# Unrolled attention with three slots for q and k, and eight-head layers in three bf16 parts

## The reference

```
attn = softmax(q @ k.T * scale)        # 1024 x 1024, no mask
out  = attn @ v                        # width 16 (8 heads) or 8 (16 heads)
```

## Time and profile before

| | us |
|---|---|
| median of 3 runs | 3769.32 |
| lowest and highest | 3768.4 and 3776.37 |
| profiled execution, own time | 3765.51 |
| its span in the profile | 3763.8 |
| PE busy in the span | 3126.6 (83%) |
| DVE busy | 2793.6 (74%) |
| ACT busy | 1868.8 (50%) |
| POOL busy | 438.7 (12%) |

### The profile page before, as it was taken

The page is one execution under the profiler, slowest core; times in us unless marked ns, Lnnn a source line. Parts: engine busy times, 40 slices in busy tenths (PEclk is TensorE's granted clock), DMA queues, the critical chain, the costliest instruction groups (busy, mean ns, idle before and its releaser), DMA issues. The chain is left out here.

```text
span 3763.8 us, 61047 instructions
## 1 busy us (share of the span) xinstructions
PE 3126.6 (83%) x19914; PEld 1782.2 (47%) x19914; DVE 2793.6 (74%) x4370; ACT 1868.8 (50%) x3233; POOL 438.7 (12%) x495
## 2 busy tenths in 40 slices
PE   6758898848888889847898979958999777759998
PEld 4533333422222223333333457656777544447776
DVE  5658877389888888547777434469999776679998
ACT  2215767517877778614767611214444444424443
POOL 0140000040000000050000001031222000032222
PEclk9857989868999999956989868859999888859999
DMA  0051212030000111041222010011111000011111
GB/s 25 15 123 25 42 29 46 5 95 16 31 30 31 33 32 40 1 95 45 46 47 46 2 24 1 0 46 46 45 45 45 4 1 0 9 52 45 45 45 53
DMA packets 74816, 131.97 MB, mean 35 GB/s; under 512 B 13872, under 2 KB 30288, under 8 KB 74576
## 3 DMA queue, kind: packets, MB, share of 16 engines
q1 hardware_dynamic: 74576, 128.75, 14.1%
HBM read 85.72 MB, written 25.43 MB: 30 GB/s over the span
## 5 line engine op out<-in xcount | busy, mean ns | idle before, releaser
L728 DVE TENSOR_REDUCE nested_a_halves<-banks 128x2 f32<-128x1024 f32 x512 | 615.9, 1222 | 132.7 <-PE banks L834 129.6
L728 DVE TENSOR_REDUCE wide_a_halves<-banks 128x2 f32<-128x1024 f32 x512 | 594.7, 1218 | 80.8 <-PE banks L834 80.5
L784 ACT ACTIVATE nested_a_p<-banks 128x512 f32<-128x512 f32 x1024 | 554.5, 597 | 201.2 <-PE banks L858 184.7
L784 ACT ACTIVATE wide_a_p<-banks 128x512 f32<-128x512 f32 x1024 | 554.1, 598 | 89.0 <-PE banks L858 66.9
L1678 ACT ACTIVATE mix_e_h<-banks,mix_b_folded 128x512 f32<-128x512 f32 x512 | 353.5, 690 | 391.8 <-PE banks L1691 383.7
L1642 DVE TENSOR_TENSOR mix_e_h_low<-mix_e_h,mix_e_h_high 128x512 fp32r<-128x512 f32 x512 | 464.0, 906 | 17.5
L834 PE MATMUL banks<-nested_k_stack,nested_q_stack 48*128 48x512 f32 x1024 | 283.0, 547 | 88.8 <-DMA nested_q_stack<-nested_q_parts 46.5
L872 PE MATMUL banks<-nested_a_p,nested_v 128*32 128x256 f32 x4096 | 345.9, 419 | 0.0
L872 PE MATMUL banks<-wide_a_p,wide_v 128*32 128x256 f32 x4096 | 333.1, 404 | 11.1 <-issue 11.1
L858 PE MATMUL banks<-nested_q_stack,nested_k_stack 50*128 50x512 f32 x1024 | 262.1, 444 | 10.1 <-ACT nested_a_p L784 9.6
L834 PE MATMUL banks<-wide_k_stack,wide_q_stack 48*128 48x512 bf16 x1024 | 211.7, 410 | 59.1 <-issue 18.5
(11 more groups left out here) (367 smaller groups left out, 4575.3 us busy)
## 6 DMA issues: line engine op xcount, KB each, us to landing
mix_e_gate<-mix_gates_t SPq DMA_DIRECT2D x128, 256.0 KB, 3.2
nested_q_stack<-nested_q_parts SPq DMA_DIRECT2D x96, 128.0 KB
nested_q_parts<-nested_p_q_cut SPq DMA_DIRECT2D x16, 512.0 KB
nested_k_parts<-nested_p_k_cut SPq DMA_DIRECT2D x16, 512.0 KB
nested_k_stack<-nested_k_parts SPq DMA_DIRECT2D x32, 256.0 KB
nested_v<-nested_values SPq DMA_DIRECT2D x16, 512.0 KB, 10.1
wide_v<-wide_values SPq DMA_DIRECT2D x16, 512.0 KB, 3.0
wide_q_stack<-wide_q_parts SPq DMA_DIRECT2D x192, 32.0 KB
```

The costliest lines, as they stand in the source:

```text
L728: dve.tensor_reduce(halves[:, half, i, 2 * a:2 * a + 2], bank[:, at:at + 2, :], AX, ALU.max).then_inc(maxed, 1)
L784: act.activation(p[:, kt % 4, j, :], bank[:, ST + n % RING, :], ACT.Exp, scale=scale).then_inc(probs, 1)
```

## The change

The loops of the attention stage become straight code over all units. `q_stack` and `k_stack` get three slots, the tile `v` and its copies go, and PE reads the values from `values`. SP loads group u/2 + 2 at the even unit u once all shifted scores of the units before u are done, and issues `shift_load(u)` behind it. The nested layers use bf16 in three parts: `pairs = [3, 2, 1]` with a width of 16 is 96 rows, 98 with the shift rows, so the span becomes 128, `per_tile` 1 and `slabs` 4. A load is then 3 + 6 = 9 DMAs per group in the nested layers, 18 in the wide one (before: 10 and 18, and one for `v`).

```diff
 class Heads:
     GROUP = 4
+    SLOTS = 3
...
-        self.q_stack = core.sbuf(ctx, "q_stack", [P, 2, self.slabs, T], kind)
-        self.k_stack = core.sbuf(ctx, "k_stack", [P, 2, self.slabs, T], kind)
-        self.v = core.sbuf(ctx, "v", [P, 2, TILES, self.GROUP * 32])
+        self.q_stack = core.sbuf(ctx, "q_stack", [P, self.SLOTS, self.slabs, T], kind)
+        self.k_stack = core.sbuf(ctx, "k_stack", [P, self.SLOTS, self.slabs, T], kind)
...
-                src = self.k_parts[bass.ds(n, 1), :, h, 0:count].rearrange("o s c e t -> (c e) (o s) t")
+                src = self.k_parts[n, :, h, 0:count].rearrange("s c e t -> (c e) s t")
...
-        sp.dma_start(self.v[:, k], self.values[:, bass.ds(n, 1)].rearrange("p o i c -> p (o i) c")).then_inc(
-            self.v_in[k], 16)
...
-                sp.wait_ge(v_copied, 2 * hd.groups)
-                for k in range(2):
-                    hd.load(sp, k, k)
+                for n in range(2):
+                    hd.load(sp, n)
...
-                shift_load(0, 0)
                 sp.wait_ge(hd.parts_out, 32 * hd.parts * B)
-
-                def turn(it, first, last):
-                    for ui in range(4):
-                        u, k = it * 4 + ui, ui // 2
-                        if ui % 2 == 0 and not (first and k == 0) and not (last and k == 1):
-                            sp.wait_ge(mixed, u * TILES)
-                            hd.load(sp, it * 2 + k + 1, (k + 1) % 2)
-                        if not (last and ui == 3):
-                            shift_load(u + 1, ui + 1)
-
-                turns(sp, hd.total // 2, turn)
+                hd.load(sp, 2)
+                for u in range(UNITS):
+                    if u >= 2 and u % 2 == 0 and u // 2 + 2 < hd.total:
+
+                        sp.wait_ge(shifted, u * ITEMS)
+                        hd.load(sp, u // 2 + 2)
+                    shift_load(u)
...
+                def shifted_scores(u, n):
+
+                    kt, j = n // 4, n % 4
+                    if n == 0:
+                        pe.wait_ge(shift_in, (u + 1) * SHIFT_LOADS)
...
+                            for n in range(4 * kt + 2 * h + RING, 4 * kt + 2 * h + 2 + RING):
+                                if n < ITEMS:
+                                    shifted_scores(u, n)
+                                elif u + 1 < UNITS:
+                                    shifted_scores(u + 1, n - ITEMS)
...
-            lambda: heads_layer(core, "nested1", 8, nested, True, F32R),
+            lambda: heads_layer(core, "nested1", 8, nested, True, BF16),
             lambda: heads_layer(core, "wide", 16, wide, False, BF16),
-            lambda: heads_layer(core, "nested2", 8, nested, True, F32R),
+            lambda: heads_layer(core, "nested2", 8, nested, True, BF16),
```

More of the change, by code:

```diff
@@ L387, in rows_of, with load @@
         return slice(base, base + self.rows + extra), j // self.per_tile
-    def load(self, sp, n, k):
+    def load(self, sp, n):
+        k = n % self.SLOTS
         for h in range(self.per_tile):
@@ L659, in attend_stage @@
     scale = float(D) ** -0.5
-    LOADS, qk_in, v_in = hd.LOADS, hd.qk_in, hd.v_in
-    q_stack, k_stack, v = hd.q_stack, hd.k_stack, hd.v
+    LOADS, SLOTS, qk_in = hd.LOADS, hd.SLOTS, hd.qk_in
+    q_stack, k_stack = hd.q_stack, hd.k_stack
     scored, maxed, top_made, high_made, shifts_made = (
@@ L681, in special_place, with slot, loaded @@
         return (17 * u + 10) % 2 * 2
+    def slot(u):
+        return u // 2 % SLOTS
+    def loaded(u):
+        return (u // 2 // SLOTS + 1) * 16 * LOADS
     with ExitStack() as ctx:
@@ L753, in _ @@
                 for m in range(PAIRS):
-                    maximum(0, 0, m)
+                    maximum(0, m)
                 shifts(0)
                 for m in range(PAIRS // 2):
[L757 to L774, removed]
+                    maximum(1, m)
+                for u in range(UNITS):
+                    if u + 1 < UNITS:
+                        for m in range(PAIRS // 2, PAIRS):
+                            maximum(u + 1, m)
+                        shifts(u + 1)
+                    for m in range(PAIRS // 2):
+                        if m == 2 and u:
+                            write_mixed(u - 1, special_place(u))
+                        if u + 2 < UNITS:
+                            maximum(u + 2, m)
+                write_mixed(UNITS - 1, special_place(UNITS))
             @block.scalar
@@ L833, in scores, with turn_shifts @@
                         rows, slab = hd.rows_of(2 * a + h)
-                        last = pe.matmul(bank[:, at + h, :], q_stack[rows, k, slab, q_at:q_at + P],
-                                         k_stack[rows, k, slab, half * BANK:(half + 1) * BANK], start=True, stop=True)
+                        last = pe.matmul(bank[:, at + h, :], q_stack[rows, slot(u), slab, q_at:q_at + P],
+                                         k_stack[rows, slot(u), slab, half * BANK:(half + 1) * BANK],
+                                         start=True, stop=True)
                     last.then_inc(scored, 1)
-                def turn_shifts(u, at):
+                def turn_shifts(u):
                     pe.wait_ge(shifts_made, u + 1)
                     for i in range(4):
-                        last = pe.matmul(bank[0:8, at + 1, i * P:(i + 1) * P],
+                        last = pe.matmul(bank[0:8, special_place(u - 1) + 1, i * P:(i + 1) * P],
                                          shift[:, i].rearrange("p c j -> p (c j)"),
@@ L851, in turn_mix @@
                     last.then_inc(mix_turned, 1)
-                def shifted_scores(u, kt, k, qc, j):
-                    n = 4 * kt + j
-                    wait_for_bank(u, n)
-                    rows, slab = hd.rows_of(j, 2)
-                    pe.matmul(bank[:, ST + n % RING, :], k_stack[rows, k, slab, kt * P:(kt + 1) * P],
-                              q_stack[rows, k, slab, qc * T2:(qc + 1) * T2], start=True, stop=True).then_inc(shifted, 1)
-                def wait_for_bank(u, n):
+                def shifted_scores(u, n):
+                    kt, j = n // 4, n % 4
+                    if n == 0:
+                        pe.wait_ge(shift_in, (u + 1) * SHIFT_LOADS)
@@ L863, in wait_for_bank @@
                     last = n - RING if n >= RING else max(range(n, ITEMS, RING)) - ITEMS
                     wait_past(pe, probs, u * ITEMS + (last + 1))
-                def mix_values(s, kt, k, c):
+                    rows, slab = hd.rows_of(j, 2)
+                    pe.matmul(bank[:, ST + n % RING, :], k_stack[rows, slot(u), slab, kt * P:(kt + 1) * P],
+                              q_stack[rows, slot(u), slab, u % 2 * T2:(u % 2 + 1) * T2],
+                              start=True, stop=True).then_inc(shifted, 1)
@@ L943, in turns @@
+                for c in range(2):
+                    mix_values(UNITS - 1, TILES - 1, c)
+                wait_past(pe, written, UNITS - 2)
+                turn_mix(UNITS - 1)
 def turns(engine, count, turn):
```

168 lines of the change are left out of this document (68 added, 100 removed).

## The result

| | before | after |
|---|---|---|
| median of four runs each, same chip | 3768.9 us (3755.0 to 3776.4) | 4026.5 us (4022.4 to 4027.1) |
| ratio, 95% interval | | 1.069 [1.065, 1.072] |
| span of the profiled execution | 3763.8 us | 4020.7 us |
| mean granted clock | 0.853 | 0.848 |

The forecast was 4055 (3930 to 4175), slower with 0.91. The turn of the shifts, once per unit (L842 before, L834 after), cuts both spans into the same seven pieces.

The account below looks back on a forecast made before the run. PE, the longest lane in both attention stages, and its waits were taken as the bound. Wide +114 and each nested layer +86 gave +286, 4051.5 us, or 4055 as median of runs; range 3930 to 4175.

Parts of the forecast that it names:

- the 23 waits: PE waits for shift rows queued behind a load on SP: 13 in the wide stage, 5 in each nested one.
- Order on SP, wide: Wide stage: shift rows issued behind 18 load DMAs hold up PE, 13 events of 13.6 us, 177 us.
- Order on SP, nested: Each nested attention: shift rows behind nine load DMAs hold up PE, five events of 13.7 us, 68.5 us.
- I take 10.3: Nested event before the clock's 3.4 us: issue and transfer ahead of the shift rows, 10.3 us, between 7.1 and 15.2.
- Unrolling and slots: Attention stages: loop returns and load waits go, -65 us in the wide stage, -51 per nested layer.
- Full array: Nested units: heads no longer side by side, unit 26.0 us, +65.6 over 15 units, +1.2 for the first.
- Head, tail and projection: Each nested layer: start and end of attention +4.8 us; projection -3, with longer fill against shorter DVE wait.
- 1: Rival: the load does not hold up the shift rows, all 23 events vanish, 3741 us; 6%.
- Rival 2: Nested attention: the full array costs nothing, the unit stays 21.6 us, 3915 us in all; 4%.
- Rival 3: Attention units: straight code stalls for code every four units as loop returns did, 4112 us; 12%.
- rival 4: Shift-row events: nested loads as slow as now and the clock falls for longer, 4123 us; 14%.
- rival 5: Shift-row events are mostly paid back as ACT and DVE restart with free banks, half price, 3900 us; 4%.

Follow-up runs that it names:

- experiment 1: Kernel after the change, with SP issuing the shift rows of a unit ahead of the load: 3706.2 us, ratio to before 0.983.
- experiment 5: Kernel after the change, with the nested layers back in fp32r: 3979.1 us in one execution, then 3957.8 us in rounds, ratio 1.046.
- experiment 9: Kernel with the shift rows ahead of the load, bf16 key slots' ones filled as 32-bit pairs, half the elements: 3693.9 us, ratio 0.981.

## Why the prediction was right

Direction and mechanism were right: the 23 waits came where they were forecast, in the number that was forecast, and moving one line took them away. Several sizes were off. The sum was +286 on the profiled execution and the trace has +257; the wide layer with its start was forecast at +114 and measured at +94.2, and 7.6 us came off at the end. The two nested layers came out nearly exactly, +172 forecast and +170.4 measured, and that is luck: against the forecast their events cost 18.7 us more, the full array 41.4 less, unrolling and slots gained 8.9 less, and their start cost 12 more.

- *Order on SP, wide: +177 forecast, +155.4 measured* (after against experiment 1). The event is 12.0 us, 9.9 of wait and 2.1 of clock, where 10.7 and 2.9 stood; no row was given for the 2.9. The issues are shorter than in the earlier trace rows, 6.2 us instead of 6.95, and PE goes on 1.6 us after the last row's issue began, where 1.9 stood. The lower bound of 11.5 was added up wrong; with its own terms it is 5.4 + 1.8 + 1.9 + 2.9 = 12.0, and the event lies on it.
- *Order on SP, nested: +68.5 forecast, +77.6 and +78.1 measured.* The event is 15.4 us: 13.1 of wait, 2.3 of clock, where 3.4 stood without a row. The term that was mis-sized is "I take 10.3". The rows landed only with the end of the load, near the upper bound of 15.2; the copy of the values behind its load had pointed to it. Smaller packets are indeed no slower, but that is worth 0.6 us (13.7 us of wait with 4 KB in experiment 5), not 4.9. What the new load is really spared is the copy: the 14.2 us of today were 2 MB on the move, 13.7 us of packets, against 1.5 MB and 10.7 us now. The rule of the Trainium skill (DMA: Bandwidth & Descriptors, Queues, rings and completion order) by which the small DMA might finish first would have given less still; the trace shows no more of it than the 0.3 us by which the rows' last packet (374.8 us) ended before the load's (375.0).
- *Unrolling and slots: -65 forecast for the wide stage, -59.4 measured; -51 for each nested one, -47.2 and -45.9 measured.* The quiet wide unit is 20.5 us, not 20.2 to 20.3, over 31 units some 6 us. In the nested stage a row was misread: "six of 5.4 us" takes the longest of the earlier trace rows for each, but six waits of 24.1 us in all make 4.0 on average. Five of them last 4.3 to 5.4 us, and a unit with one takes 28.6 us, which is 6.6 above the quiet 22.0 of straight code and not 7.8. That the total came near is again in part luck: the unit with the loop return takes 32.2 us, and the units without an event took 22.5 to 22.8 us before and take 22.0 now, which the forecast had left out.
- *Full array: unit 26.0 and +66.8 per layer with its slow first unit forecast, 25.34 and +45.3, +46.9 measured.* The step was right within 0.02 us (1.56 against 1.54). The unit was forecast 4.4 us above the one it replaces and is 3.3 above it. Of the difference 0.7 us lie in the unit itself, half of that in the step, and 0.4 in the base: fp32r units in straight code take 22.0, not 21.6. The Trainium skill (TensorE: Matmul & The Clock Gate, Wait - 56ns, not 53.3ns?) had 215.7 ns from start to start, from which the prediction estimated 1.53 for the step and 25.5 for the unit; the trace agrees, with 0.44 us per pair, 1.54 and 25.34.
- *Head, tail and projection: +4.8 - 3 forecast, +7.8 measured before each nested layer (the tail lies elsewhere).* The growth of the fill came in full (10.36 us) and is on the path, as experiment 9 shows. DVE's wait did shrink, from 24.4 us to 14.1, but that did not pay for the fill and the third part. How the 7.8 us are made up beyond the fill is not shown; before the second nested layer, where the same code takes 191.1 to 199.2 us, they are less sure than before the first.

```profile
251.41 0.69 DVE L551 CAST nested_p_q_cut<-nested_p_q_t 128x1024 bf16<-128x1024 f32 x1 [14.09 <-DMA nested_k_parts<-nested_p_k_cut]
```

  The wide head came out at -1.8 instead of +2.
- *Not in the forecast: -7.6 us behind the last nested turn.* The same 253 matmuls of the last unit, first of the kernel before, then after:

```profile
2114.30:2154.40 40.10, 36.23 (x253) 12.78 (x248) 2.81 (x8) 24.38 (x46) 0.00 (x0) 0.70 0.01 1
```
```profile
2378.90:2409.30 30.40, 26.54 (x253) 8.39 (x248) 2.81 (x8) 24.07 (x46) 0.00 (x0) 1.00 0.01 1
```

Before, the clock fell in it; after, it did not. PE is busy 9.7 us longer before, and the granted clock is 0.70 against 1.00. The first nested layer has 1.00 in both. What made it fall there is not shown.

Of the rivals, 1 was ruled out by the waits and is what experiment 1 made true (3706 against the 3741 it gave). Rival 2 by the unit. Rival 3 did not come: the three `PEq` waits are one per layer, at its start, and none follows in the units; the kernel before has the same three (7.4, 8.8 and 7.3 us, against 10.0, 9.8 and 10.3 after). Of rival 4 the slow nested loads came more than half of the way (13.1 us of wait between 10.3 and 15.2), the longer clock not in this kernel. Of rival 5 nothing was seen: every event costs more than its wait.

## What to carry to other kernels

When a load is moved within a queue, list what else that queue carries in the same unit and who waits for it: a bulk load ahead of a few small rows that PE's next matmul needs made a 59 us gain a 257 us loss, and one line swapped gave it back. Price such a place twice, by the issues ahead and by the bytes ahead, and take the larger; giving the small transfer a queue of its own did not help here once the bulk was moving, issuing it first did. And judge the parts of a change apart: unrolling, the earlier loads and the values in place gained 152 us (a third slot had little part in it), the full array of the nested layers cost 92.

## What the runs showed of the hardware

- Two DMAs of 4 KB issued from GpSimd's queue behind 1.5 MB on SyncE's landed after 8.8 us in the event shown, against 1.6 us alone, and PE waited no less than with the rows on the same queue (13.05 and 13.1 us).
- After waits of about 13.7 us in fp32r units TensorE's clock stayed at the lower level for 37.5 us, to the end of the unit, in four of ten, in both executions profiled, and for 17 to 20.5 us in the others; in the bf16 units of the kernel of the change, with waits of 12.3 to 15.0 us, it was at the lower level for 13.6 to 17 us.
- Load packets of 4 KB and of 2 KB moved 1.5 MB in about the same time, 11.0 and 10.7 us.
- GpSimd's fill goes by elements: the same bytes took 10.36 us as 12288 bf16 and 5.24 us as 6144 fp32 elements per partition.
